# Graph attention with gathered keys: key transposes two tiles ahead, two score banks, two query banks, and one bank for adj and probability transposes

## The reference

```
q = x @ Wq.T + bq;  k = key @ Wk.T + bk;  v = value @ Wv.T + bv      # 4096 x 512 each
scores = q @ k.T / sqrt(4096) * adj                                  # adj is 0/1, 4096 x 4096, sparse
scores = where(abs(scores) < 1e-5, -1e9, scores)
y = x + softmax(scores) @ v @ Wm.T + bm
out = layernorm(y)                                                   # no gain, no bias
```

## Time and profile before

| | us |
|---|---|
| median of 3 runs | 458.14 (457.96 to 459.02) |
| span of the profiled execution | 486.1 |
| PE busy in the span | 444.0 (91%) |
| DVE busy | 317.3 (65%) |
| ACT busy | 191.2 (39%) |
| POOL busy | 248.6 (51%) |

### The profile page before, as it was taken

One profiled execution on the slowest core, in us unless ns is written; L12 is line 12 of the kernel. 1 busy time (PEld: TensorE's weight loads), 2 busy tenths in 40 slices (PEclk: granted clock), 3 DMA queues, 4 the chain that ended last, 5 costly groups with the idle time before them and its releaser, 6 DMA issues.

```text
span 486.1 us, 5650 instructions
## 1 busy us (share of the span) xinstructions
PE 444.0 (91%) x1536; PEld 246.8 (51%) x1536; DVE 317.3 (65%) x923; ACT 191.2 (39%) x447; POOL 248.6 (51%) x251
## 2 busy tenths in 40 slices
PE   9999999999999889999889798998979899889982
PEld 5444444444444455666455465655645455555651
DVE  0258535993487067989997685976937675435684
ACT  1232413433341433434443353453444345335573
POOL 2110005007672166877777776766766666661410
PEclk9999999999999998999999899999989999998997
DMA  8999999999999999998999866999757566562553
GB/s 329 363 221 285 283 290 257 226 267 316 332 311 343 268 281 241 248 285 242 229 239 321 267 188 241 257 249 324 200 150 245 166 204 227 165 212 80 156 188 112
DMA packets 34693, 119.25 MB, mean 245 GB/s; under 512 B 6767, under 2 KB 7023, under 8 KB 32610
## 3 DMA queue, kind: packets, MB, share of 16 engines
q0 software_dynamic: 18480, 70.45, 57.6%
q1 hardware_dynamic: 12866, 28.51, 16.4%
q10 hardware_dynamic: 3312, 19.89, 10.3%
HBM read 139.78 MB, written 17.56 MB: 324 GB/s over the span
## 4 chain that ended last, share of the span: by engine, by line
PE 63%; DVE 14%; another core or an unknown queue 8%; ACT 8%; issue 6%; ACTq 0%; DVEq 0%
PE bank L584 23%; PE bank L594 15%; PE bank L713 8%; PE bank L737 5%; PE bank L635 3%; PE bank L647 3%; PE bank L694 3%; ACT keyT L922 2%; DVE stats L1296 2%; ACT y_buf L969 2%; ACT qT L906 2%; DVE big L1077 1%; PE bank L724 1%; DVE score L1261 1%
## 5 line engine op out<-in xcount | busy, mean ns | idle before, releaser
L594 PE MATMUL bank<-big,M 128*128 128x472 f32 (+1 forms) x288 | 125.0, 562 | 8.4 <-ACT qT L906 7.4
L584 PE MATMUL bank<-y_buf,big 128*128 128x512 f32 x256 | 111.6, 594 | 0.7 <-ACT y_buf L881 0.7
L481 POOL DMA_INDIRECT v_g<-table,index x70 | 73.6, 1052 | 70.2 <-PE bank L737 20.6
L470 POOL DMA_INDIRECT key_g<-key,index x70 | 75.8, 1082 | 21.4 <-issue 21.4
L713 PE MATMUL bank<-keyT,qT 128*118 128x256 f32 x280 | 70.8, 398 | 15.1 <-ACT keyT L922 8.5
L492 POOL DMA_INDIRECT adj_g<-adj_cols,index x70 | 71.3, 1018 | 21.3 <-issue 21.3
L594 PEld LDWEIGHTS bank<-big,M 128*128 128x128 f32 x288 | 52.9, 195 | 57.1 <-issue 43.2
L584 PEld LDWEIGHTS bank<-y_buf,big 128*128 128x128 f32 x256 | 48.1, 190 | 59.4 <-issue 57.9
L713 PEld LDWEIGHTS bank<-keyT,qT 128*118 128x118 f32 x280 | 51.5, 188 | 42.1 <-ACT keyT L922 16.9
L461 POOL DMA_DIRECT2D big<-adj_tiles x35 | 19.9, 571 | 103.2 <-PE bank L584 68.1
L1077 DVE TENSOR_TENSOR big<-big 128x1888 bf16<-128x1888 bf16 x35 | 39.8, 1138 | 42.0 <-DMA big<-adj_tiles 42.0
(11 more groups left out here) (124 smaller groups left out, 510.5 us busy)
## 6 DMA issues: line engine op xcount, KB each, us to landing
big<-adj_tiles POOLq DMA_DIRECT2D x35, 944.0 KB
x_buf<-x SPq DMA_DIRECT2D x35, 256.0 KB
out<-y_buf SPq DMA_DIRECT2D x34, 256.0 KB
big<-valueT ACTq DMA_DIRECT2D x8, 1024.0 KB
big<-xT SPq DMA_DIRECT2D x7, 944.0 KB
table<-qT ACTq DMA_DIRECT2D x5, 1024.0 KB
table<-y_buf ACTq DMA_DIRECT2D x3, 1024.0 KB
big<-xT ACTq DMA_DIRECT2D x2, 944.0 KB
```

The lines of the kernel that those rows point to most:

```text
L470: pool.indirect_dma_start(key_g[:, b, c, :], None, key, bass.IndirectOffsetOnAxis(index[:, t, c:c + 1], 0), bounds_check=N - 1, oob_is_err ...
L481: pool.indirect_dma_start(v_g[:, b, c, :], None, table, bass.IndirectOffsetOnAxis(index[:, t, c:c + 1], 0), bounds_check=N - 1, oob_is_err ...
L584: mm = nc.tensor.matmul(bank[4 + t % 2][:, :], col_buf[nb % 2][:, d, k * P:(k + 1) * P], G[:, d, :], start=(d == 0), stop=(d == DC - 1))
L594: mm = nc.tensor.matmul(ps[:, 0:n], M[:, d, a * P:(a + 1) * P], xT_buf[nb % 2][:, d, 0:n], start=(d == 0), stop=(d == DC - 1))
```

## The change

- A second buffer for transposed keys and one for transposed adj, used by even tiles, in free columns of `big`.
- TensorE's step i now holds: `keys(i+2)`; `scores(i+1)` here already if i is above 30; all of `values_of(i)`; the first half of the query unit; `scores(i+1)` if i is up to 30; list matmuls as before; the second half of the unit; `adj_transposes(i+2)`; `prob_transposes(i)`.
- Scores of even tiles go to bank 3, of odd ones to bank 2. They wait for the soften two tiles back.
- Query units go to bank 7 or, in odd steps outside the list steps and outside step 29, to bank 6; the first half waits for the copy of the last unit on the same bank.
- Transposes of adj (from tile 2 on) and of probabilities share bank 4.
- ScalarE, step i up to 30: `sizes(i)`, `exps(i)`, then the copies of the last step's query unit and probabilities, of adj i+1 and of keys i+2.
- Before the loop, keys of tile 0 and adj of tiles 0 and 1 are transposed ahead of the last of the five first query units, and keys of tile 1 ahead of the first scores.
- Semaphores: one for keys, one for scores, one for probability transposes, in place of two shared ones; GpSimd's gathers wait on these.

```diff
+        keyT_spare = big[:, 15488:15488 + DC * SLOTS].rearrange("p (a k) -> p a k", a=DC)
+        adjT_spare = big[:, 15488 + DC * SLOTS:15488 + (DC + 1) * SLOTS]
...
+        keyT_buf = (keyT_spare, keyT[:, :, :])
+        adjT_buf = (adjT_spare, adjT[:, :])
...
+        prob_half = bank[4][:, 0:CH * R]
+        def score_bank(t):
+            return bank[3 - t % 2][0:R, 0:SLOTS]
+        def adj_half(t):
+            return bank[2][0:R, t * SLOTS:(t + 1) * SLOTS] if t < 2 else bank[4][0:R, SLOTS:2 * SLOTS]
+        def in_lists(i):
+            return list_step(i)[0] is not None
+        def unit_bank(i):
+            return 6 if i % 2 and not in_lists(i) and i != COUNTS + 1 else 7
+        def unit_before(i):
+            return max((AHEAD + k for k in range(i) if unit_bank(k) == unit_bank(i)), default=None)
...
 def gather_keys(t):
-                    pool.wait_ge(keyT_adjT_ps, t - KD + 1)
+                    pool.wait_ge(keyT_ps, t - KD + 1)
 def gather_adj(t):
-                if t >= AD:
-                    pool.wait_ge(keyT_adjT_ps, t - AD + 1)
+                if t >= AD + 2:
+                    pool.wait_ge(probT_ps, t - AD - 1)
+                elif t >= AD:
+                    pool.wait_ge(keyT_ps, 1)
...
 def adj_transposes(t):
-                if t >= 1:
-                    pe.wait_ge(adjT_sb, t)
+                if t == 2:
+                    pe.wait_ge(q_sb, AHEAD)
+                if t >= 3:
+                    pe.wait_ge(adjT_sb, t)
+                    pe.wait_ge(probT_sb, t - 2)
...
 def scores(t):
-                if t >= 1:
-                    pe.wait_ge(prod_sb, t)
+                if t == 1:
+                    pe.wait_ge(adjT_sb, 2)
+                if t >= 2:
+                    pe.wait_ge(prod_sb, t - 1)
...
 TensorE's loop
-                if i + 1 < T:
-                    keys(i + 1)
-                    adj_transposes(i + 1)
-                if values_of(i):
-                    values(values_of(i)[0])
+                if i + 2 < T:
+                    keys(i + 2)
+                if LAST_QUERY < i < T - 1:
+                    scores(i + 1)
+                for t in values_of(i):
+                    values(t)
                 if u is not None:
-                    pe.wait_ge(q_sb, u)
-                    project(u, bank[7], 0, 1)
-                if i + 1 < T:
+                    if unit_before(i) is not None:
+                        pe.wait_ge(q_sb, unit_before(i) + 1)
+                    project(u, bank[unit_bank(i)], 0, 1)
+                if i <= LAST_QUERY:
                     scores(i + 1)
-                if i == CATCH_UP:
-                    values(i - 1)
 ...
+                if u is not None:
+                    project(u, bank[unit_bank(i)], 2, 3)
+                if i + 2 < T:
+                    adj_transposes(i + 2)
                 if i < T:
                     prob_transposes(i)
-                if u is not None:
-                    project(u, bank[7], 2, 3)
...
 ScalarE's loop
-                if i <= LAST_QUERY:
-                    copy_keys(i + 1)
                 if i < T:
                     sizes(i)
-                    if LAST_QUERY < i < T - 1:
-                        copy_keys(i + 1)
+                    if i == CATCH_UP:
+                        copy_unit(i - 1)
+                        copy_prob(i - 1)
+                        copy_adj(i + 1)
+                    if CATCH_UP < i < T - 2:
+                        copy_keys(i + 2)
                     exps(i)
-                if i + 1 < T:
+                if 1 <= i < CATCH_UP:
+                    copy_unit(i - 1)
+                    copy_prob(i - 1)
                     copy_adj(i + 1)
+                if i <= CATCH_UP:
+                    copy_keys(i + 2)
                 if i < T - 1 and sqrt_of(i):
                     roots(i, sqrt_of(i))
-                if i < T:
+                if CATCH_UP <= i < T:
                     copy_prob(i)
-                u = q_unit(i)
-                if u is not None:
-                    copy_q(u, bank[7])
+                    if i + 2 < T:
+                        copy_adj(i + 2)
```

More of the change, by code:

```diff
@@ L601, in lists @@
                 pe.wait_ge(any_sb, START[b] + BATCH[b])
+                if b >= 2:
+                    pe.wait_ge(q_sb, max(AHEAD + k + 1 for k in range(LIST_AT[b]) if unit_bank(k) == 6))
                 if b > 2:
@@ L675, in _ @@
                     spread_slots(1)
[L676 to L686, removed]
             def keys(t):
@@ L709, in scores @@
                 pe.wait_ge(q_sb, (t // 4 + 1) * DC)
-                if t >= 1:
-                    pe.wait_ge(prod_sb, t)
+                if t == 1:
+                    pe.wait_ge(adjT_sb, 2)
+                if t >= 2:
+                    pe.wait_ge(prod_sb, t - 1)
                 for a in range(DC):
[L713 to L716, removed]
+                    mm = nc.tensor.matmul(score_bank(t), qT[:, t // 4 % QB, a, t % 4 * R:(t % 4 + 1) * R],
+                                          keyT_buf[t % 2][:, a, :], start=(a == 0), stop=(a == DC - 1))
+                mm.then_inc(score_ps, 1)
             def prob_transposes(t):
@@ L746, in values @@
                     mm.then_inc(pv_ps, 1)
-            keys(0)
-            adj_transposes(0)
+            pe.wait_ge(v_sb, UNITS)
+            pe.wait_ge(u_sb, 1)
+            for u in range(AHEAD):
+                if u == 3:
+                    pe.wait_ge(wide_sum_sb, DC)
+                    nc.tensor.matmul(bank[6][:, :], sel_rest, rest_sum, start=False, stop=True).then_inc(spare_ps, 1)
+                if u == AHEAD - 1:
+                    keys(0)
+                    adj_transposes(0)
+                    adj_transposes(1)
+                if u >= 2:
+                    pe.wait_ge(q_sb, u - 1)
+                project(u, bank[4 + u % 2])
+            keys(1)
             scores(0)
+            pe.wait_ge(spare_sb, VD)
             for i in range(T + 1):
                 b, step = list_step(i)
-                if i + 1 < T:
-                    keys(i + 1)
-                    adj_transposes(i + 1)
-                if values_of(i):
-                    values(values_of(i)[0])
-                u = q_unit(i)
+                u = q_unit(i)
+                if i + 2 < T:
[4 more added lines that the diff above has]
+                    values(t)
                 if u is not None:
-                    pe.wait_ge(q_sb, u)
                     if i == 0:
                         pe.wait_ge(bits_sb, 2 * 2)
-                    project(u, bank[7], 0, 1)
-                if i + 1 < T:
+                    if unit_before(i) is not None:
+                        pe.wait_ge(q_sb, unit_before(i) + 1)
+                    if unit_bank(i) == 6 and any(at + STEPS <= i for at in LIST_AT.values()):
+                        pe.wait_ge(index_ready, max(b + 1 for b, at in LIST_AT.items() if at + STEPS <= i) * (2 * CH))
+                    project(u, bank[unit_bank(i)], 0, 1)
+                if i <= LAST_QUERY:
                     scores(i + 1)
-                if i == CATCH_UP:
-                    values(i - 1)
                 if step == 0:
@@ L775, in _ @@
                     pe.wait_ge(lead_sb, 2)
+                    pe.wait_ge(q_sb, max(AHEAD + k + 1 for k in range(i) if unit_bank(k) == 6))
                     for k in range(2):
@@ L907, in copy_q, with copy_keys, copy_adj @@
                                      ).then_inc(q_sb, 1)
+            def copy_keys(t):
+                act.wait_ge(keyT_ps, t + 1)
+                if t >= 2:
+                    act.wait_ge(score_ps, t - 1)
+                for c in range(CH):
+                    nc.scalar.activation(keyT_buf[t % 2][:, :, c * P:(c + 1) * P],
+                                         key_bank[c][:, :].rearrange("p (a k) -> p a k", a=DC), ACT.Copy
+                                         ).then_inc(keyT_sb, 1)
+            def copy_adj(t):
+                if t < 2:
+                    act.wait_ge(keyT_ps, 1)
+                else:
+                    act.wait_ge(probT_ps, t - 1)
+                    act.wait_ge(prod_sb, t - 1)
+                nc.scalar.activation(adjT_buf[t % 2][0:R, :], adj_half(t), ACT.Copy).then_inc(adjT_sb, 1)
             for u in range(AHEAD):
+                if u == AHEAD - 1:
+                    copy_keys(0)
+                    copy_adj(0)
+                    copy_adj(1)
                 copy_q(u, bank[4 + u % 2])
@@ L915, in _ @@
                         nc.scalar.activation(v_g[96:P, b, CH - 1, :], bank[6][96:P, :], ACT.Copy).then_inc(spare_sb, 1)
[L917 to L930, removed]
+            copy_keys(1)
             def sizes(t):
@@ L944, in copy_prob @@
             def copy_prob(t):
-                act.wait_ge(score_probT_ps, t + 2)
+                act.wait_ge(probT_ps, t + 1)
                 if t >= 2:
                     act.wait_ge(pv_ps, t - 1)
```

(12 more changed lines are left out.)

25 lines of the change are left out of this document (15 added, 10 removed).

## The result

The changed kernel takes 464.49 us (median of 4 runs, 464.01 to 465.77); the kernel before took 458.05 us beside it (4 runs, 457.87 to 459.02). The ratio is 1.0131, with an interval of 1.0094 to 1.0168: the change costs 6.4 us. The prediction was 464.7.

A forecast was written before the change was run, and what follows sets the result against it. TensorE's own work of 7.92 us a step was taken as the bound, VectorE bounding steps 5 to 8. Terms -3.0 + 2 x 2.5 + 1.5 + 1.4 + 1.7 + 0 = +6.6 us on 458.1 gave 464.7, range 460 to 468.

The forecast's parts named there:

- The late marks: Eleven steps from 9 to 28 with "remote" waits, about 29 us in the profiled execution; timed executions hardly have them.
- Start and steps 0 to 9, −3.0: Loop start through step 9: VectorE 5.7 us sooner, 2.4 and some 0.3 given back; net -3.0 us.
- Stalls of 2.5, 1.5, 2.5 and 1.4 us: Steps 10, 14, 18, 22: TensorE's first half of a unit waits for the query copy behind late exponentials.
- One clock drop, +1.7: Behind one of the two 2.5 us stalls, steps 10 or 18, the clock halves: +1.7 us (0 to 3.4).
- End, 0: End of the loop: scores running ahead gain, late soften at step 30 costs; taken as zero (-2 to +1).
- Scores on two banks: Scores wait for an earlier soften, so the 2.29 us at step 1 and 1.66 at step 6 lose their cause.
- The signs: Profile after: unit waits in steps 10, 14, 18, 22; scores not waiting for key copies; keys never waiting.
- The rival "faster": Key copies' slack and early scores pay, under 3 us of the four stalls appears: 447 to 457, say 454; chance 0.17.
- The rule named beside it: Independent matmul groups should rotate through banks so one's copy overlaps the next group; alone it would give 454 us.

The follow-up runs named there:

- experiment 1: The kernel before, with no edit, profiled a second time: 457.8 us, span 456.0 us.
- experiment 6: The changed kernel with all scores on bank 3, waiting for the soften one tile earlier: 465.96 us, ratio to before 1.016.
- experiment 8: The kernel before with ScalarE's key copies moved behind the size, without a second key buffer: 457.43 us, ratio to before 0.998.
- Experiment 2: The changed kernel with ScalarE's copy of the last query unit moved ahead of the size: 452.18 us, ratio to before 0.984.
- Experiment 5: The changed kernel, unit copy still late, units alternating on banks 6 and 7, lists on bank 2, all scores on bank 3: 455.35 us, ratio to before 0.993.
- experiment 4: The changed kernel with the unit copy ahead of the size and every query unit on bank 7: 452.44 us, ratio to before 0.987.
- experiment 7: The kernel before with ScalarE's query unit copy moved behind the exponentials of the next step: 526.68 us, ratio to before 1.149.

## Why the prediction was right, step by step

In spans the change costs 462.1 less 456.0, 6.1 us; timed it is 6.4. The forecast's sum was 6.6. Its terms:

- *The late marks.* Right: they are absent in experiment 1, and after's span is below that of the first profile of before although the kernel is slower.
- *Start and steps 0 to 9, −3.0.* Measured −4.1. TensorE and VectorE in the second profile of before:

```profile
182.81 3.52 PE L713 MATMUL bank<-keyT,qT 128*118 128x256 f32 x8 [2.28 <-DVE score L1254]
...
255.38 0.40 PE L724 MATMUL bank<-cst,score 118*128 118x118 f32 x2
255.62 1.76 PE L594 MATMUL bank<-big,M 128*128 128x472 f32 x4
257.21 1.04 PE L694 MATMUL bank<-cst,key_g 128*128 128x128 f32 x8
258.08 0.38 PE L704 MATMUL bank<-cst,adj_g 128*118 128x128 f32 x2
...
263.33 0.37 PE L724 MATMUL bank<-cst,score 118*128 118x118 f32 x2
```

```profile
243.82 0.48 DVE L1254 SCALAR_TENSOR_TENSOR score<-bank,c_cols,adjT 118x256 f32<-118x256 f32 x1
```

  The same work is done before at 258.30, where values follow the adj transposes of 258.08, and after at 254.21. VectorE's soften of tile 8 moved from 243.82 to 237.20 (after's trace), 6.6 us where the forecast said 5.7; so 2.5 us were given back, against 2.4 and 0.3. The 0.9 us that were missing are spread out: VectorE's first soften came 1.7 us sooner (forecast 1.5), step 0 gave 1.6 (1.4), steps 1 to 5 gave 3.3 (2.8). The waits for size in steps 0 and 2 to 5 are gone as forecast; after's trace has none before the loop's end. Each kernel has one clock drop in this stretch, before behind the 2.28 us of the first row, after behind the 2.26 of step 7; the forecast had neither, and they cancel.
- *Stalls of 2.5, 1.5, 2.5 and 1.4 us.* Measured as idle time 2.22, 1.03, 2.19 and 0.85, in exactly these steps. As lengthened steps, against the second profile of before: 10.40 less 7.95 is 2.45 at step 10; the same difference is 1.4 at step 14, 4.1 at step 18 with its clock drop, 1.15 at step 22. The chain of durations held: soften 4.05 us behind scores (255.80 less 251.75; forecast 4.03), copy ready 7.4 us behind them (259.18 less 251.75) where 7.5 was worked out from the earlier trace rows. As idle time the stalls are 0.3 to 0.6 us shorter than forecast: the copy let TensorE go on 3.2 to 3.4 us behind soften and not 3.5, and idle time counts from the end of the row before, some 0.2 us behind the sum of starts that the forecast used.
- *One clock drop, +1.7.* Right in number for steps 10 and 18: one of the two, in the profiled execution here and in that of experiment 6. Which of them it is the runs didn't settle. That the longer stalls draw it, as the forecast took from the earlier trace rows, doesn't hold: it fell behind 1.88 us in experiment 8 and 2.19 here, and not behind 2.22 here or 2.75 in experiment 8.
- *End, 0.* Too low: the terms above leave +1.1 of the 6.1, just above the +1 that it was given as its upper bound. After's trace has VectorE's last probabilities late there, TensorE idling 1.08, 1.16 and 0.94 us for them in steps 32 to 34. All of TensorE's waits behind step 30 come to 4.1 us there against 2.7 in the second profile of before. No experiment tested it.
- *Scores on two banks.* The waits of the earlier trace rows for soften are gone, but the adj transposes on the shared bank take 1.38 us at step 1 instead, which the prediction had inside its −3.0.
- *The signs.* No scores wait for a key copy any more, as the prediction named it. Keys were to wait never and wait once, 0.41 us in step 2, for a ScalarE copy and not for a gather.

The sum came out 0.2 us from the median partly by errors that cancel: 1.1 us too little gain ahead of step 10, 0.5 us too much loss in the four steps (9.6 for 9.1), 1.1 us too little loss at the end. That is luck in the number; the place and the cause of the loss were right.

Experiment 2 prices the two sides apart. With the copy early the change gains 6.0 us (458.15 to 452.18), so the late copy costs 12.3 (to 464.49). The forecast's terms are 5.7 of gain, and 9.6 + 2.7 = 12.3 of loss. So close an agreement is luck in part too, as experiment 2 has waits and clock drops of its own.

The rival "faster" fell with its conditions: the late marks are not in timed runs (experiment 1), and the four stalls hold 6.3 us, not less than 3. The rule named beside it did better. The Trainium skill, "Perfetto Trace Analysis", section "Optimizing Tensor Performance", asks for that rotation so that a group's evacuation overlaps the next group. Experiment 5 bears it out, 455.35 for 464.49 us; experiments 2 and 4, 452.18 and 452.44 us, show that with the copy placed early the rotation has nothing left to give that can be told.

## What to carry to other kernels

When a copy that frees a matmul bank is moved behind other work on an in-order engine, take the latest arrival of that work in any step, not the usual one, and compare it with the time at which TensorE comes back to the bank. Before giving a group a second bank, look whether the copying engine idles ahead of the copy: here one call moved ahead of two others was worth 12.3 us (464.49 to 452.18), a second bank on top of it nothing that can be told. And, as experiments 7 and 8 suggest, keep transposes far enough ahead before their copies are put behind anything.

## What the runs showed that was not expected

- One profiled execution of the kernel before carried 30 us that a second one didn't have (spans 486.1 and 456.0). A span above the timed median is a reason to profile again before any row of it is priced.
- The clock drop behind stalls of the same length moves from one place to another between kernels that differ little: 2.22 us without and 2.19 with it in the kernel after, 2.23 with and 2.20 without it in experiment 6. Length alone doesn't decide: in experiment 8 there was a drop behind 1.88 us and none behind 2.75, in experiment 2 one behind 1.53 and 0.41. A drop should be priced as a chance.
- The faster kernel meets a transfer that the slower ones hid: in experiment 2 VectorE waited at step 11 for the load of x (in experiment 4 such a wait took 4.2 us; the other profiles have none). VectorE of that kernel:

```profile
264.06 0.75 DVE L1260 CUSTOM_DVE_ANT_0 big<-x_buf,w_row,kappa 118x512 f32<-118x512 f32 x1 [2.28 <-DMA x_buf<-x]
```
